# A gated cross attention and expert layer: second normalisation, routing and shared expert taken apart by batch

## The reference

```python
x = x + tanh(g_xattn) * (attention(layernorm(x), ctx) @ W_proj + b_proj)
xn = layernorm(x)
logits = xn @ gate_w.T                       # 8 experts
topk_logits, topk_idx = top_k(logits, 2)
w = softmax(topk_logits)
out = sum over the two experts e of w_e * ((silu(xn @ wg[e].T) * (xn @ wu[e].T)) @ w_down[e].T)
shared = (silu(xn @ sg_gate.T) * (xn @ sg_up.T)) @ sg_down.T
x = x + tanh(g_ffn) * (shared + out)
```

## Time and profile before

| | us |
|---|---|
| median of 3 executions | 592.05 (591.93 to 593.0) |
| profiled execution | 597.62 |
| its span | 594.4 |
| busy in the span: PE, DVE, ACT, POOL | 531.9, 304.4, 233.4, 140.5 |
| mean granted clock of TensorE | 0.946 |

### The profile page before, as it was taken

The page is one execution under the profiler, slowest core; times in us unless marked ns, Lnnn a source line. Parts: engine busy times, 40 slices in busy tenths (PEclk is TensorE's granted clock), DMA queues, the critical chain, the costliest instruction groups (busy, mean ns, idle before and its releaser), DMA issues.

```text
span 594.4 us, 8011 instructions
## 1 busy us (share of the span) xinstructions
PE 531.9 (89%) x2393; PEld 285.8 (48%) x2393; DVE 304.4 (51%) x611; ACT 233.4 (39%) x430; POOL 140.5 (24%) x169
## 2 busy tenths in 40 slices
PE   0899777999999999996989999899999999999980
PEld 0455312333333333332449656456777777777750
DVE  4375793788778787873447441223333333333320
ACT  2344314777777777773653211011221221222210
POOL 7073000000110000100000046711333333333332
PEclk9999856999999999998998599999999999999995
DMA  8237990565565267374000013322333433333322
GB/s 282 80 97 252 243 363 38 152 177 154 165 183 151 78 206 206 104 232 118 11 2 0 2 57 128 136 89 73 61 63 53 64 63 54 56 65 59 54 27 26
DMA packets 52654, 65.73 MB, mean 111 GB/s; under 512 B 6800, under 2 KB 44432, under 8 KB 52112
## 3 DMA queue, kind: packets, MB, share of 16 engines
q1 hardware_dynamic: 33440, 39.84, 23.7%
q0 software_dynamic: 7152, 9.34, 9.6%
q10 hardware_dynamic: 12032, 16.17, 8.5%
HBM read 37.93 MB, written 27.20 MB: 110 GB/s over the span
## 4 chain that ended last, share of the span: by engine, by line
PE 65%; DMA 12%; DVE 8%; SPq 5%; issue 4%; ACT 2%; ACTq 1%; POOLq 0%; DVEq 0%; POOL 0%
PE ps L852 51%; PE ps L920 9%; DMA out<-unit_region 8%; DVE neg_max L658 3%; DMA unit_region<-nm_parts 2%; SPq L296 2%; SPq L286 2%; DVE slot_rows L607 2%; PE ps L1141 1%; DMA gates<-in_g_ffn 1%; PE ps L1121 1%; ACT ctx_region L513 1%; PE ps L928 1%; DVE unit_region L834 1%; PE ps L1031 1%
## 5 line engine op out<-in xcount | busy, mean ns | idle before, releaser
L658 DVE TENSOR_REDUCE neg_max<-ps 128x2 f32<-128x1024 f32 x128 | 150.9, 1219 | 43.2 <-PE ps L852 43.2
L513 ACT ACTIVATE ctx_region<-ps 128x512 f32<-128x512 f32 x256 | 141.4, 596 | 76.8 <-PE ps L852 75.6
L852 PE MATMUL ps<-unit_region 96*128 96x512 bf16 (+1 forms) x512 | 147.0, 401 | 18.8 <-DMA unit_region<-nm_parts 8.6
L852 PEld LDWEIGHTS ps<-unit_region 96*128 96x128 bf16 (+1 forms) x512 | 46.2, 99 | 134.2 <-ACT ctx_region L513 67.8
L852 PE MATMUL ps<-up_region,unit_region 128*128 x312 | 107.1, 486 | 0.0
L437 POOL DMA_INDIRECT out<-unit_region x39 | 60.6, 1553 | 138.1 <-DMA out<-unit_region 77.8
L852 PE MATMUL ps<-dn_region,unit_region 128*128 (+1 forms) x330 | 78.4, 380 | 3.3 <-issue 2.7
L852 PEld LDWEIGHTS ps<-dn_region,unit_region 128*128 128x128 f32 x330 | 62.5, 190 | 21.7 <-issue 5.3
L852 PEld LDWEIGHTS ps<-up_region,unit_region 128*128 128x128 f32 x312 | 56.2, 190 | 31.0
L920 PE MATMUL ps<-ctx_region,unit_region 128*32 128x512 f32 x512 | 69.9, 619 | 0.7 <-ACT ctx_region L513 0.7
L826 DVE TENSOR_TENSOR unit_region<-unit_region,ps 128x384 f32<-128x384 f32 x39 | 21.6, 554 | 77.2 <-ACT unit_region L572 74.3
(11 more groups left out here) (118 smaller groups left out, 454.0 us busy)
## 6 DMA issues: line engine op xcount, KB each, us to landing
up_region<-in_w_upT ACTq DMA_DIRECT2D x9, 768.0 KB, 4.3
qk_parts<-up_region SPq DMA_DIRECT2D x32, 192.0 KB, 5.3
unit_region<-qk_parts SPq DMA_DIRECT2D x32, 192.0 KB, 4.3
x_slots<-empty ACTq DMA_DIRECT2D x1, 5031.0 KB, 18.4
unit_region<-x_slots SPq DMA_DIRECT2D x39, 129.0 KB
v_rows<-dn_region SPq DMA_DIRECT2D x4, 1024.0 KB, 6.6
unit_region<-qk_parts SPq DMA_DIRECT2D x32, 128.0 KB, 4.3
unit_region<-v_rows SPq DMA_DIRECT2D x16, 256.0 KB, 4.6
```

Source lines behind the costliest of these rows:

```text
L513: nc.scalar.activation(probs[:, k % 8, :], bank(4 + k % 2), ACT.Exp).then_inc(exp_done, 1)
L658: nc.vector.tensor_reduce(neg_max[:, s, 2 * p:2 * p + 2], bank(2 * (p % 2), 2), AX.X, ALU.max, negate=True).then_inc(max_done, 1)
L852: return nc.tensor.matmul(o_, w, m, start=start, stop=stop)
```

## The change

The output projection gets eight steps in slot 14, at every second one (`also_first`), and five in slot 15, at steps 0 to 4 (`also_last`). Slot 15 also takes for batch 0 the transposes, the router and a transpose of the logits, at steps 8, 10 and 12. The last four tiles go by pairs: the two banks 6 and 7 hold both their transposes and their products.

The second layer norm is made batch by batch. The square root leaves ScalarE: VectorE's `rstd2` computes the inverse root in 13 dependent instructions from a starting value by integer operations and three refinements. The copies to `xnT` go from ScalarE to VectorE but for one of batch 3.

The router is turned round: the gate weights, widened with zeros to 32 columns, are stationary, the tokens are streamed, and the four tiles of a batch go to the four 32-column groups of one bank; the result is copied and transposed back (`turn_logits`). Largest and index are taken per batch (`top_of`).

The shared expert is cut into twelve pieces `n` (batch x chunk), each into gate and up half and by chunks of the channels, and the first four pieces and batch 0's down product are laid between the last batch's projection, normalisation and routing. The routing from the chosen experts on is the same, but for the order of two copies, and the second part of the rank sum waits behind one tile of a down product and not behind `shared_up`. SyncE's program and GpSimd's behind attention are the same.

The work areas and banks (extracts):

```diff
+        unit_pair = 2 * HG * T // 2
+
+        def home(word):
+            assert used[0] <= word
+            used[0] = word
+
...
+        logits = work(NT * E, "p (t e) -> p t e", t=NT)
+        logitsT = work(2 * P, "p (s n) -> p s n", s=2)
...
         def bank(i, n=1):
             return ps[i // 4][:, i % 4, :] if n == 1 else ps[i // 4][:, i % 4:i % 4 + n, :]
 
+        def attn_bank(t, first):
+            n = t % TB
+            return (bank(first + t % 2)[:, 0:D] if t < NT - TB else bank(6 + n // 2)[:, n % 2 * D:(n % 2 + 1) * D])
+
         def turned(t):
...
+            return attn_bank(t, 0)
 
         def projected(t):
...
+            return attn_bank(t, 2)
 
         def rowsT_bank(b, c):
...
+            return bank(2 * b + c)
+
+        def shared_bank(i, q):
+            return bank((4 if i == 0 else 6) + q)
+
+        def logit_bank(b):
+            return bank((0, 5, 4, 6)[b])
```

GpSimd and ScalarE at the start, ScalarE behind attention:

```diff
+            nc.gpsimd.memset(gate_sb[:, :, :], 0.0).then_inc(gate_zero, 1)
+            pool.wait_ge(gate_zero, 1)
             nc.gpsimd.memset(empty[:, :], 0.0).then_inc(const_step, 1)
...
-            act.dma_start(gate_sb[:, :, :], gateT.rearrange("(c p) n -> p c n", p=P)).then_inc(small_in, 16)
+            act.wait_ge(gate_zero, 1)
+            act.dma_start(gate_sb[:, :, 0:E], gateT.rearrange("(c p) n -> p c n", p=P)).then_inc(small_in, 16)
...
+
+            def copy_logitsT(b):
+                act.wait_ge(logitT_ps, b + 1)
+                nc.scalar.copy(logitsT[:, b % 2, :], logit_bank(b)[:, 0:P]).then_inc(logitT_sb, 1)
+
+            for q in range(2):
+                act.wait_ge(atT_ps, NT - TB + 2 * q + 2)
+                nc.scalar.copy(attnT[:, 2 * q:2 * q + 2, :, :], bank(6 + q).rearrange("p (t c n) -> p t c n", t=2, c=DC)
+                               ).then_inc(atT_sb, 2)
+            shared_silu(0)
+            copy_logitsT(1)
+            copy_logitsT(2)
+            shared_silu(1)
+            shared_silu(2)
+            act.wait_ge(rowsT_ps, 2 * B)
+            nc.scalar.copy(xnT[:, 1, N - T:N], rowsT_bank(B - 1, 1)).then_inc(rowsT_odd, 1)
+            copy_logitsT(3)
+            shared_silu(3)
+            act.wait_ge(route, 4)
             nc.scalar.activation(pexp[:, 1, :], pexp[:, 0, :], ACT.Exp).then_inc(pexp_done, 1)
...
+            for n in range(4, FC * B):
+                shared_silu(n)
```

VectorE, new helpers and the new order:

```diff
+            roots = [0]
+
+            def root_of(ins):
+                roots[0] += 1
+                ins.then_inc(root_step, 1)
+                dve.wait_ge(root_step, roots[0])
+
+            def rstd2(b):
+                tiles = slice(b * TB, (b + 1) * TB)
+                v, y, a = std[:, tiles], rstd[:, tiles], root_a[:, tiles]
+                dve.wait_ge(var_done, B + b + 1)
+                root_of(nc.vector.tensor_scalar(v, mean_var[:, tiles, 1], EPS, None, ALU.add))
+                root_of(nc.vector.tensor_scalar(a.bitcast(I32), v.bitcast(I32), 1, None, ALU.logical_shift_right))
+                root_of(nc.vector.tensor_copy(y, a.bitcast(I32)))
+                root_of(nc.vector.tensor_scalar(y.bitcast(I32), y, -1.0, float(ROOT_START), ALU.mult, ALU.add))
+                for _ in range(3):
+                    root_of(nc.vector.scalar_tensor_tensor(a, y, -0.5, y, ALU.mult, ALU.mult))
+                    root_of(nc.vector.tensor_tensor(a, a, v, ALU.mult))
+                    root_of(nc.vector.scalar_tensor_tensor(y, a, 1.5, y, ALU.add, ALU.mult))
+
+            def apply2(b):
+                for t in range(b * TB, (b + 1) * TB):
+                    last = nc.vector.tensor_scalar(rows[:, t, :], x_sb[:, t, :], mean_var[:, t, 0:1],
+                                                   rstd[:, t:t + 1], ALU.subtract, ALU.mult)
+                last.then_inc(rows_done, 1)
+
+            def copy_rowsT(b, chunks=range(DC)):
+                dve.wait_ge(rowsT_ps, B + b + 1)
+                for c in chunks:
+                    last = nc.vector.tensor_copy(xnT[:, c, b * T:(b + 1) * T], rowsT_bank(b, c))
+                last.then_inc(rowsT_sb, 1)
+
+            def copy_logits(b):
+                dve.wait_ge(logit_ps, b + 1)
+                nc.vector.tensor_copy(logits[:, b * TB:(b + 1) * TB, :],
+                                      logit_bank(b)[:, P:2 * P].rearrange("p (t w) -> p t w", w=GW)[:, :, 0:E]
+                                      ).then_inc(logit_sb, 1)
+
+            def top_of(b):
+                dve.wait_ge(logit_sb, b + 1)
+                for t in range(b * TB, (b + 1) * TB):
+                    last = nc.vector.max(top8[:, t, :], logits[:, t, :])
+                last.then_inc(top_done, 1)
+                dve.wait_ge(top_done, b + 1)
+                for t in range(b * TB, (b + 1) * TB):
+                    last = nc.vector.max_index(top8_idx[:, t, :], top8[:, t, :], logits[:, t, :])
+                return last
+
+            def shared_hidden(n):
+                dve.wait_ge(sh_silu, n + 1)
+                if n >= FC:
+                    dve.wait_ge(sh_y_ps, n // FC * 2)
+                nc.vector.tensor_tensor(sh_hT[:, n % FC, :], sh_gate[:, n % FC, :], bank(2 * (n % 2) + 1), ALU.mult
+                                        ).then_inc(sh_hid, 1)
 
             def shared_added(i):
                 for q in range(2):
                     dve.wait_ge(sh_y_ps, 2 * i + q + 1)
                     dst = x_sb[:, i * TB + 2 * q:i * TB + 2 * q + 2, :]
...
+                    nc.vector.scalar_tensor_tensor(dst, shared_bank(i, q).rearrange("p (t d) -> p t d", t=2),
                                                    tanh_g[:, 1:2], dst, ALU.mult, ALU.add).then_inc(sh_added, 1)
 
+            for t in range(5):
+                residual(t)
+            stats2(0)
+            residual(5)
+            normalise(UNITS - 3, B - 1, NG - 3)
+            residual(6)
+            rstd2(0)
+            residual(7)
+            apply2(0)
+            for t in range(8, NT - TB + 1):
+                residual(t)
+            copy_rowsT(0)
+            stats2(1)
+            normalise(UNITS - 2, B - 1, NG - 2)
+            dve.wait_ge(logitT_ps, 1)
+            nc.vector.tensor_copy(logitsT[:, 0, :], logit_bank(0)[:, 0:P]).then_inc(logitT_sb, 1)
+            rstd2(1)
+            apply2(1)
+            copy_logits(0)
+            stats2(2)
+            rstd2(2)
+            apply2(2)
+            normalise(UNITS - 1, B - 1, NG - 1)
+            copy_rowsT(1)
+            copy_rowsT(2)
+            shared_hidden(0)
+            for q in range(2):
+                t = NT - TB + 2 * q
+                dve.wait_ge(proj_ps, t + 2)
+                nc.vector.scalar_tensor_tensor(x_sb[:, t:t + 2, :], bank(6 + q).rearrange("p (t d) -> p t d", t=2),
+                                               tanh_g[:, 0:1], x_sb[:, t:t + 2, :], ALU.mult, ALU.add
+                                               ).then_inc(x1_done, 2)
+            stats2(3)
+            rstd2(3)
+            apply2(3)
+            shared_hidden(1)
+            copy_rowsT(3, range(1))
+            shared_hidden(2)
+            copy_logits(1)
+            copy_logits(2)
+            for b in range(B - 1):
+                top_of(b)
 
...
+            copy_logits(3)
+            step(top_of(3))
             step(nc.vector.tensor_tensor(pexp[:, 0, :], top8[:, :, 1], top8[:, :, 0], ALU.subtract))
...
+            for i in range(1, B):
+                shared_hidden(FC * i)
+                shared_added(i - 1)
+                shared_hidden(FC * i + 1)
+                shared_hidden(FC * i + 2)
```

TensorE:

```diff
             def project(t):
-                pe.wait_ge(atT_sb, t + 1)
+                pe.wait_ge(atT_sb, t + 1 if t < NT - TB else t - t % 2 + 2)
                 for c in range(DC):
...
             def turn_rows(b):
                 pe.wait_ge(rows_done, B + b + 1)
...
+                if b == 0:
+                    pe.wait_ge(atT_sb, NT - TB)
                 elif b == 1:
...
+                    pe.wait_ge(x1_done, NT - TB)
+                elif b == 3:
+                    pe.wait_ge(x1_done, NT)
                 for t in range(TB):
                     for c in range(DC):
                         last = nc.tensor.transpose(rowsT_bank(b, c)[:, t * P:(t + 1) * P],
...
                 last.then_inc(rowsT_ps, 1)
 
             def router(b):
...
+                if b == 3:
+                    pe.wait_ge(rowsT_odd, 1)
+                pe.wait_ge(rowsT_sb, B + (b if b != 1 else 2) + 1)
+                for c in range(DC):
+                    for t in range(TB):
+                        tok = b * T + t * P
+                        last = nc.tensor.matmul(logit_bank(b)[t * GW:(t + 1) * GW, 0:P], gate_sb[:, c, :],
+                                                xnT[:, c, tok:tok + P], start=c == 0, stop=c == DC - 1,
+                                                skip_group_check=True)
+                last.then_inc(logitT_ps, 1)
+
+            def turn_logits(b):
+                pe.wait_ge(logitT_sb, b + 1)
```

(83 more changed lines are left out.)

197 lines of the change are left out of this document (41 added, 156 removed).

## The result

The changed kernel takes 602.44 us (median of 4 executions, 599.75 to 604.86) where the kernel before, run beside it, takes 592.27 (591.93 to 593.0): ratio 1.0169, 95% interval 1.0123 to 1.0215. It is 10 us slower. The forecast was slower, 596.3 us, range 589.8 to 600.5; the time lies above the range.

What follows compares the result with a forecast made beforehand. Two chains, TensorE's shared expert and routing plus scatters, end within some 5 us; the later counts. First scatter +5.1 gives block transpose +2.2, clock adds 2.0: +4.2 on the median 592.05, hence 596.3 us, range 589.8 to 600.5.

Steps and rivals of the forecast that it cites:

- Slots 14 and 15: End of attention: added projections, transposes and router lengthen the two slots by 2.9 and 3.0 us, to 315.9.
- Last normalisation: VectorE's program order before the last unit's normalisation makes it start at 322.1, 10.7 us later than before.
- Choice and first scatter: Choice of experts at 346.7, +8.0 us; 5.6 us from there, so first scatter at 352.3, +5.1 us.
- Block transpose and clock: First block transpose at 399.9, +2.2 us; TensorE idles 11 us before it, then half clock costs 2.0 us.
- (b): TensorE's clock also falls between 322 and 343 us, costing 3.5 us more: 599.8 us; chance 0.18.
- (c): VectorE's backlog is smaller, first scatter earlier; a gain if that is before 347.18 + 0.95; chance 0.20.
- (d): The delays and the block load's wait cancel: no change, 592.05 us; chance 0.12.
- last scatter to block transpose: Between last scatter and first block transpose, 2.95 us of waiting in the kernel before would vanish.
- 38 output intervals: Accumulating scatters to the output behind the first block: 38 intervals of 4.56 us, unchanged.
- the base: Block transpose at 399.9 against the profiled 397.7, +2.2 us; the total carried over to the median, 592.05 us.
- doubt in the base: Unprofiled executions may already have the block transpose near 394.75; then the loss is 7.1 us: 599.2 us.
- the end: Behind the first block nothing changes; whatever moves the start of the blocks moves the end by as much.

Runs made afterwards that it cites:

- short root: Changed kernel with the inverse root's three refinements left out, 4 steps in place of 13: median 598.83 us, ratio 1.0005 to the kernel before.
- clean pair: Kernel before and changed kernel, both unaltered, on one chip without late notices: medians 592.66 and 601.58 us, ratios 0.9999 and 1.016.
- clean chip: Chip on which both unaltered kernels ran without late notices: before 592.66 us, changed 601.58 us.
- first set's chip: Chip of the first follow-ups: kernel before again 604.33 us, ratio 1.0104; changed kernel again 600.82 us, ratio 1.0051.
- stores late: Changed kernel with the stores of batches 1 and 2 moved behind the loads of blocks 0 and 1: 601.19 us, ratio 1.0154.
- half the scatters: Either kernel without the 16 scatters of the second choice: before 589.97 us, ratio 0.9922; changed 585.88 us, ratio 0.9869.
- fifth set: Identity transposes added at TensorE's start: 24 in the kernel before, 595.84 us; 16 or 30 in the changed kernel, 599.76 and 599.8 us.
- An edit that removes slack on TensorE: Changed kernel with the last shared down product ahead of the first block transpose: 603.76 us on one chip, 594.41 us on another.
- the store late: Kernel before with the store of batch 2 moved behind the loads of blocks 0 and 1: 592.36 us, ratio 1.0004.

## Why the prediction was off, step by step

**Slots 14 and 15, 1.3 us more than forecast.** The last attention product runs from 316.15 to 317.2, forecast end 315.9. The router came near its lower bound: 0.65 us for 16 records, where I took 1.2. The prediction worked out that lower bound, 0.5 us, as the time by the rule of the Trainium skill (TensorEngine Tiling (Array Packing), Key Properties) that different tiles load and multiply in parallel, and the trace agrees with the rule rather than with my middle value.

**Last normalisation, right.** 322.68 against 322.1, with VectorE never idle from 310.4; 13 steps of 0.2 us. Two misses cancel in part: the normalisation of unit 14 began at 312.17 instead of 310.9, and what stands from there to the last took 10.5 us instead of 11.2. The short root confirms that this order, not TensorE, sets it: 1.8 us less per root, three times, took it from 322.26 to 316.94.

**Choice and first scatter, right within 1.3 us.** Choice done 345.5 against 346.7; from there to the scatter 5.5 against 5.6; first scatter 351.04 against 352.3. On the clean pair it is +4.2 where I forecast +5.1.

**Block transpose and clock, right.** 398.70 against 399.9, an idle stretch of 10.90 us against 11, and the clock at 0.50 behind it. The down product took 7.21 us where 24 such products take 5.45: 1.8 against my 2.0. On the clean chip it took 6.61, 1.2 more.

**Rivals.** (b) is refuted: the clock was 1.00 from 322 to 338.5. (c) and (d) too: no version of the changed kernel had its first scatter at 348.1 or before but the short root. Only on the first set's chip, where before itself takes 599 to 607 us, do the medians leave no loss.

**Where the sum fails.** In the prediction's terms, with the clean pair beside it:

| term | forecast | clean pair |
|---|---|---|
| first scatter | +5.1 | +4.2 |
| train of the 32 scatters | 0 | +1.4 |
| last scatter to block transpose | -2.9 | -0.75 |
| block transpose to block product | +2.0 | +0.8 |
| 38 output intervals | 0 | +2.8 |
| sum | +4.2 | +8.5 |

**The first step that failed is the base**: "+2.2 us" for the block transpose, and "the median of the runs shown is 592.05, hence 596.3". The prediction counts the change as gaining 2.9 us behind the last scatter, where before's load waited for a store and TensorE for a late result. That wait was in the profiled execution and is not in every one: without late notices before needs 5.52 us from last scatter to block transpose and not 9.0, and there is 0.75 to gain. The prediction named this as its "doubt in the base" and gave 599.2 us for it, but put the number on the other side. The row to weigh was "381.35 2.67 issue": a stretch of the bounding engine that no program order explains, and a load that waited for a store whose sums TensorE had finished. It was carried over as if every execution had it. The changed kernel waits 10.9 us for its block and so neither pays for late notices nor gains where there are none; its profile (603.1) and median (602.4) agree.

Late notices are not all of what was high in before's profile. Against the profile of the clean chip it takes 5.04 us more: 3.0 between first scatter and block product, with the late notices; 0.9 up to the first scatter, where its clock was lower (last section); 1.4 outside the span; and 0.4 less in the outputs.

**The second is the end**: "Whatever moves the start of the blocks moves the end by as much", with 38 intervals of 4.56 us and 41.5 us of scatters for both kernels. On the clean pair the 38 intervals are 2.8 us longer, the largest single miss, and the train 1.4. The four profiles of the changed kernel unaltered show 4.66, 4.634, 4.651 and 4.644 us; the four of before 4.561, 4.642, 4.572 and 4.571. Whether the pace belongs to the changed kernel stays open: before had 4.642 once, and kernels that differ from the changed one little (stores late, half the scatters) had 4.57 and 4.58. What the runs show is that the excess lies in intervals in which a transfer of instructions falls.

The first scatter and the clock were forecast 2.1 us too dear, which hides part of both misses. All terms together move the forecast by 4.3 us, to 600.6. The last 1.8 us to 602.44 are in no row: the first comparison has 10.2 us between medians, the clean pair 8.5 between profiles and 8.9 between medians.

**What differs between chips** is before more than after. Before's medians in the four comparisons are 592.27, 606.94, 593.6 and 592.04 us, those of after 602.44, 600.82, 598.9 and 601.58; the ratio is smallest, 1.0051, where before's own profile has late notices. These go with the chip more than with the kernel: all seven profiles of the first and the fifth set have them, none of the eleven of the other three, and of the first two profiles that of before. All late notices lie beside scatters; what makes a notice late was not found.

## What to carry to other kernels

Two chains ended close to each other (on the clean chip TensorE waited 0.56 us for its block), and the change shortened the one that could no longer gain anything, TensorE's: work laid between the steps of the path that starts the serial scatters delayed all that followed, while TensorE got 11 us of slack that it could not use. Before adding dependent small instructions to an engine, look at which transfer stands behind that engine's last result.

When a profiled execution lies above the median, find what makes it so before carrying the difference over, outside the span too: a wait that no program order explains may belong to the execution or the chip, and a kernel with slack there will not pay for it. Compare such a pair on several executions, with a profile each.

An edit that removes slack on TensorE gained 4.5 us on one chip, and on another, with late notices, its median was 2.9 us higher: slack in front of a wait is also a cover. And time one program against itself on each chip: here that ratio was 0.9999 on one and 1.0104 on another.

## What the runs showed of the hardware

- Waits of ScalarE and VectorE lasted up to 17.27 us; what they waited for had been ready for 9.7 us in the case of before's silu at 391.07. All began while GpSimd issued its 32 scatters, and profiles without such waits start each silu within 0.1 us of its product's end from the first scatter on.
- The same program on one chip ran between 593 and 613 us over 26 executions, on three others between 587 and 598, and on that of the fifth set between 592 and 609, with one execution at 705 and a mean clock of 0.743.
- The kernel before has a clock stretch of its own between 318 and 338.5 us that varies between executions, and its first scatter comes the earlier the higher it is: mean granted clock 0.59 in its first profile with the first scatter at 347.18, 0.67 in its fourth with 346.25, 0.83 with the store late and 345.08. With half the scatters it was 0.75. The changed kernel had 1.00 in all.
- Of 760 intervals between output scatters those without a transfer of instructions took 4.56 us in the mean, the 143 with one 4.81.
- An ACT table load took 1.28 us, twice between 343 and 347 us, beside VectorE's last indices and off the path.
